# Two-layer graph network on one core: the turn of x by DMA transposes of f16 halves, handed on to the second attention

## The reference

```
def _L0_gnn_ref(src, adj_matrix, ...):
    ...
    x = _ln(src + attn_out, g1, beta1)
    ff = jax.nn.gelu(x @ W1 + b1, approximate=False) @ W2 + b2
    return _ln(x + ff, g2, beta2)

def _L1_gnn_ref(features, adj, Wq, Wk, Wv, Wffn, g1, b1, g2, b2):
    q = heads(features @ Wq)
    k = heads(features @ Wk)
    v = heads(features @ Wv)
    e = jnp.einsum('whqd,whkd->whqk', q, k)
    e = jnp.where(e >= 0, e, ALPHA * e)
    attn = jax.nn.softmax(jnp.where(adj[:, None] > 0, e, NEG), axis=-1)
    h = jnp.einsum('whqk,whkd->whqd', attn, v)
    h = h.transpose(0, 2, 1, 3).reshape(w, n, H * DH)
    out = _layernorm(h, g1, b1)
    out = jnp.concatenate([out, features], axis=-1) @ Wffn.T
    out = _layernorm(out, g2, b2)
    return out + features
```

## Time and profile before

| | us |
|---|---|
| median of 3 runs | 3217.97 |
| lowest, highest | 3217.51, 3224.02 |
| the profiled execution | 3219.48 |
| its span in the trace | 3217.7 |
| stretch of the feed-forward (first load to last store) | 1197 to 1919 |
| stretch of the second attention | 1922 to 3217 |

### The profile page before, as it was taken

How to read it: one execution, slowest core, us unless ns; L and a number is a source line. 1 busy time by engine, 2 the same in 40 slices (tenths; PEclk the granted TensorE clock), 3 DMA queues, 4 the chain that set the end, 5 groups by cost and what they waited for, 6 DMA issues and landing times. The chain is left out here.

```text
span 3217.7 us, 75464 instructions
## 1 busy us (share of the span) xinstructions
PE 3034.0 (94%) x27976; PEld 2081.9 (65%) x28165; DVE 2451.6 (76%) x6789; ACT 1998.5 (62%) x3727; POOL 1679.2 (52%) x1510
## 2 busy tenths in 40 slices
PE   6999999999999949999999977999999999999996
PEld 4666666666666626666666655777777777777774
DVE  5888888888888855565555545888888888888883
ACT  3566656656666535566556644777777777777774
POOL 1555545555555542344344442666666666666665
PEclk8999999999999979999999989999999999999998
DMA  5444444444444421111111113444444444444441
GB/s 156 140 133 136 141 129 147 128 142 134 136 140 134 135 73 37 46 53 49 44 53 53 40 60 121 138 133 146 140 137 142 133 141 142 142 140 133 140 135 45
DMA packets 290744, 365.69 MB, mean 114 GB/s; under 512 B 31680, under 2 KB 199232, under 8 KB 290368
## 3 DMA queue, kind: packets, MB, share of 16 engines
q1 hardware_dynamic: 289216, 359.25, 36.5%
q10 hardware_dynamic: 1152, 1.52, 0.2%
HBM read 242.16 MB, written 118.49 MB: 112 GB/s over the span
## 5 line engine op out<-in xcount | busy, mean ns | idle before, releaser
L2445 DVE TENSOR_TENSOR f_gl<-f_act,f_gh 128x512 f16<-128x512 f32 x256 | 245.3, 959 | 285.2 <-ACT f_act L2367 285.2
L1844 ACT ACTIVATE b_prob<-b_score_t 128x512 f32<-128x512 f32 x512 | 304.2, 594 | 248.5 <-PE b_score_t L2107 248.4
L2034 DVE CUSTOM_DVE_ANT_0 b_junk<-b_score,b_mask 128x256 bf16<-128x256 f32 x1024 | 390.2, 418 | 40.8 <-issue 40.6
L1408 DVE TENSOR_TENSOR a_linked<-a_prob,a_mask 128x1024 f32<-128x1024 f32 x256 | 356.5, 1393 | 2.3 <-ACT a_prob L1205 2.2
L1928 POOL TENSOR_TENSOR b_half_sum<-b_prob 128x512 f32<-128x512 f32 x256 | 335.3, 1310 | 43.6 <-ACT b_prob L1844 43.4
L2362 ACT ACTIVATE f_gh<-f_up,s_f_b 128x512 f16<-128x512 f32 x256 | 175.5, 685 | 280.4 <-PE f_up L2493 280.3
L1205 ACT ACTIVATE a_prob<-a_score_t 128x1024 f32<-128x1024 f32 x256 | 259.3, 1013 | 109.6 <-PE a_score_t L1488 102.7
L1916 POOL TENSOR_TENSOR b_nw_root<-b_nw_var,b_minus_halves 128x2 f32<-128x2 f32 x128 | 112.9, 882 | 407.0 <-DVE b_nw_neg_mean L1975 407.0
L1401 DVE TENSOR_REDUCE a_neg_max<-a_score 128x4 f32<-128x1024 f32 x256 | 307.1, 1199 | 3.9 <-PE a_score L1501 3.8
L1850 ACT ACTIVATE b_score_t<-b_score_t 128x512 f32<-128x512 f32 x512 | 305.8, 597 | 0.3 <-PE b_score_t L2116 0.3
L2491 PE MATMUL f_down<-s_w,f_gh 128*128 128x256 f16 x1024 | 279.1, 273 | 1.0 <-DVE f_gl L2445 1.0
(11 more groups left out here) (235 smaller groups left out, 9205.3 us busy)
## 6 DMA issues: line engine op xcount, KB each, us to landing
a_stack<-qk_scratch SPq DMA_DIRECT2D x384, 128.0 KB, 3.0
b_stack<-qk_scratch SPq DMA_DIRECT2D x384, 128.0 KB, 2.8
qk_scratch<-a_qk SPq DMA_DIRECT2D x64, 512.0 KB, 2.9
qk_scratch<-b_qk SPq DMA_DIRECT2D x64, 512.0 KB, 2.8
a_x_sb<-x_t SPq DMA_DIRECT2D x64, 256.0 KB, 3.2
a_adj_sb<-adj_t SPq DMA_DIRECT2D x64, 256.0 KB, 3.1
a_res<-x_nodes SPq DMA_DIRECT2D x64, 256.0 KB, 3.4
after_attention<-a_z_out SPq DMA_DIRECT2D x64, 256.0 KB, 2.5
```

Source lines behind the costliest of these rows:

```text
L1408: nc.vector.tensor_tensor(linked[:, k], prob[:, k], mask[:, be[1] % 2].unsqueeze(1).to_broadcast([P, 2, NT * N]), ALU.mult).then_inc(link_ ...
L1844: nc.scalar.activation(prob[:, he], score_t[s][:].rearrange("p t n -> p (t n)"), ACT.Exp, scale=ALPHA).then_inc(exp_done, 1)
L2034: last = nc.vector.tensor_tensor_reduce(junk[:, s, it], score[s][:, it], mask[:, i, it], -1.0, 3e38, ALU.add, ALU.min, neg_max[:, i, col:c ...
L2445: nc.vector.tensor_tensor(gl[:, bu[1] % 2, f], act32[:, f % 2], gh[:, bu[1] % 2, f], ALU.subtract).then_inc(low_done, 1)
```

## The change

In the feed-forward, x is no longer turned on PE. ACT makes the high half of the unturned x in SBUF (`xnh`, slot 1) and DVE the low half (`xnl`, slot 1), both laid out as 8 blocks of 128x128. SP turns each with one DMA transpose (128 x 1024, f16, SBUF to SBUF) into `xh` and `xl`. x is loaded one step earlier than before. PE waits at slot 0 for both transposes.

A stage is added to the pipeline (bz, t-4; 36 steps instead of 35). In it ACT and DVE split the result z_out into halves (`znh`, `znl`, slot 2), SP turns them with two more DMA transposes into `zt`, waits for these and stores `zt` in two DMAs to a new HBM tensor, after_layer_0_turned. The f32 result is still stored.

The second attention loads this tensor (256 KB for a batch, both halves) straight into `x_halves` at 4, and has no xT, xh and xl. q waits for the load and for the v of the batch before. The sum of an out row that used a turn bank (`turn[0]`) has a PSUM bank of its own, and one small copy moved on DVE.

```diff
-    AT = {"load": 4, "load_adj": 4, "xT": 8, "xh": 8, "xl": 9, "q": 10, "q_hi": 10, ...
+    AT = {"load": 4, "load_adj": 4, "q": 10, "q_hi": 10, ...
...
-                        if (n := after(back(bx, XS), 4, 1)) is not None:
-                            sp.wait_ge(proj_done, n)
-                        sp.dma_start(x_sb[:, i], rows(x_in, bx)).then_inc(x_loaded[i], 16)
+                        if (n := after(back(bx, XB), 1, 1)) is not None:
+                            sp.wait_ge(out_done, n)
+                        sp.dma_start(x_halves[:, bx[1]].rearrange("p k c n -> p k (c n)"), x_turned[number(bx)]).then_inc(x_loaded[i], 16)
...
-                    if bx := due(t, h, "xT"):
...
-                                pe.wait_ge(xl_ready, count(bp, 1, 1))
+                                pe.wait_ge(x_loaded[bp[1] % XS], uses(bp, XS) * 16)
+                                if (n := after(back(bp, 1), 1, 1)) is not None:
+                                    pe.wait_ge(v_ready, n)
...
@@ feed_forward, SP @@
+                for bl in ((bx, back(t, -1)) if number(t) == 0 else (back(t, -1),)):
+                    if have(bl):
+                        i = bl[1] % 4
+                        if (n := after(back(bl, 4), 1, 1)) is not None:
+                            sp.wait_ge(xb_ready, n)
+                            sp.wait_ge(xnl_ready, n)
+                        sp.dma_start(x_sb[:, i].rearrange("p (g t) n -> p g (t n)", g=G), pair_rows(x_in, bl)).then_inc(x_loaded[i], 16)
                 if have(bx):
-                    i = bx[1] % 4
-                    if (n := after(back(bx, 4), 1, 1)) is not None:
-                        sp.wait_ge(xb_ready, n)
-                    sp.dma_start(x_sb[:, i].rearrange("p (g t) n -> p g (t n)", g=G), pair_rows(x_in, bx)).then_inc(x_loaded[i], 16)
+                    i = bx[1] % 2
+                    if (n := after(back(bx, 2), FC, FC)) is not None:
+                        sp.wait_ge(up_done, n)
+                    sp.wait_ge(xnh_ready, count(bx, 1, 1))
+                    sp.dma_start_transpose(xh[:, i].rearrange("p d n -> p (d n)").rearrange("p (g n) -> p g n", n=P),
+                                           xnh[:, i].rearrange("p d t n -> p (d t n)")).then_inc(x_turned[i], 16)
+                    sp.wait_ge(xnl_ready, count(bx, 1, 1))
+                    sp.dma_start_transpose(xl[:, i].rearrange("p d n -> p (d n)").rearrange("p (g n) -> p g n", n=P),
+                                           xnl[:, i].rearrange("p d t n -> p (d t n)")).then_inc(x_turned[i], 16)
+                if have(bz):
+                    i = bz[1] % 2
+                    if have(back(bz, 2)):
+                        sp.wait_ge(zt_stored[i], uses(back(bz, 2), 2) * 32)
+                    sp.wait_ge(znh_ready, count(bz, 1, 1))
+                    sp.dma_start_transpose(zt[:, i, 0]..., znh[:, i]...).then_inc(z_turned[i], 16)
+                    sp.wait_ge(znl_ready, count(bz, 1, 1))
+                    sp.dma_start_transpose(zt[:, i, 1]..., znl[:, i]...).then_inc(z_turned[i], 16)
...
                     sp.wait_ge(affine, count(bn, 2, 2))
                     sp.dma_start(pair_rows(x_out, bn), ...).then_inc(out_stored[i], 16)
+                if have(bz):
+                    i = bz[1] % 2
+                    sp.wait_ge(z_turned[i], uses(bz, 2) * 32)
+                    for k in range(2):
+                        sp.dma_start(turned_out[...], zt[:, i, k]).then_inc(zt_stored[i], 16)
...
@@ feed_forward, PE @@
-                            pe.wait_ge(xl_ready, count(bu, 1, 1))
+                            pe.wait_ge(x_turned[i], uses(bu, 2) * 32)
...
-                    if f == 4 and have(bx):
...
-                                last = nc.tensor.transpose(turn[d][:, tt * P:(tt + 1) * P], x_sb[:, bx[1] % 4, tt, d * P:(d + 1) * P], ident[:])
```

More of the change, by code:

```diff
@@ L2294, in feed_forward @@
         nw = norm_scratch(ctx, nc, "f_nw", TT)
-        turn = [psum(f"turn{i}", [P, TOK]) for i in range(DC)]
+        row = psum("row", [P, 512])
         up = [psum(f"up{i}", [P, TOK]) for i in range(2)]
@@ L2318, in run @@
         def run(eng, step):
-            for n in range(PAIRS + 3):
+            for n in range(PAIRS + 4):
                 step((n // U, n % U))
@@ L2411, in step @@
                     i = bx[1] % 4
-                    pool.wait_ge(turned, count(bx, 1, 1))
+                    pool.wait_ge(x_loaded[i], uses(bx, 4) * 16)
                     if (n := after(back(bx, 4), TT, TT)) is not None:
@@ L2523, in step @@
                         pe.wait_ge(prep, 3)
[L2524 removed]
                         for d in range(DC):
[L2526 removed]
+                            last = nc.tensor.matmul(row[:, 0:D], shift_wide[:, d], stage[:, HEADS_W, d], start=d == 0, stop=d == DC - 1)
                         last.then_inc(row_made, 1)
[L2528 to L2537 removed]
             run(pe, step)
```

126 lines of the change are left out of this document (64 added, 62 removed).

## The result

| | before | after |
|---|---|---|
| median in the paired runs, us | 3217.74 | 3195.61 |
| lowest of after, highest of after (4 runs) | | 3195.04, 3201.24 |
| ratio, 95% interval | | 0.9931 [0.9914, 0.9949] |
| span of the profiled execution | 3217.7 | 3193.5 |
| first load of the second attention, from the span's start | 1922.00 | 1901.81 |

The account below looks back on a forecast made before the run. PE was taken to bound the feed-forward and its chain the second attention. 3219.5 - 27.8 - 27.3 + 0.8 + 7.4 = 3172.6, forecast as 3171 us, 1.5% faster; likeliest range 3155 to 3195, wider range 3155 to 3400.

Parts of the forecast that it names:

- The feed-forward's turn, 27.8 us: Feed-forward: 8 transposes off PE save 0.87 us in each of 32 steps, 27.8 us; step 21.71 becomes 20.84.
- the new work of ACT and DVE is hidden: Feed-forward: ACT to some 14.4 us, DVE to 14.0 of 20.84 per step, costed at nothing; 10 us if not covered.
- c, the price of a transpose: Feed-forward: SP and queue time per DMA transpose, taken as 2 us; free in the steady state up to 4.2 us.
- rivals 1 and 2: Slow transposes make SP's queue the bound: about 3405 us at 6 us each (0.16), or about 3980 (0.14 with what lies between).
- rival 2: Each 128x128 block costs a transfer of its own, 10.4 us per transpose: about 3980 us; chance 0.14 with what lies between.
- Head +0.8 and tail +7.4: Feed-forward's ends: first up product 0.8 us later for the turned x, and 7.4 us for the added last step.
- The second attention, 27.3 us: Second attention: 4 transposes off PE save 0.44 us in each of 62 batches, 27.3 us.
- Is something late next there?: Second attention: check whether a neighbour holds PE; ACT's relu leaves 1.1 us of slack, so PE may move 0.44 us earlier.
- At the stage's head nothing is won: Second attention's start: no gain, since q is held by the mask work (adj_t, `linked`, the count), not by x.
- number 3: ACT or DVE overrun, c between 4.2 and 4.5, or relu, add and exp hold the second attention: 3195 to 3211; 0.08.
- the second attention's batch at 18.6 us: Sign of being right in the profile after: one batch of the second attention takes 18.6 us, from 19.06.
- the wait for relu (L2107, now L2094): Sign for part of the gain: in the second attention this PE wait grows by what the turn gave.

Follow-up runs that it names:

- x_only: Kernel before with only the feed-forward's x turned by DMA; z neither split nor stored turned, second attention as before: 3193.25 us, ratio 0.9903.
- turns_3x: Changed kernel with each of the four DMA transposes of a feed-forward step issued three times, the extra two into spare buffers: 3224.4 us, single run.
- after_half_late: Changed kernel where POOL's second half_sum of a batch in the second attention also waits for DVE's offset: 3179.65 us, ratio 0.9883.
- ff_all: Changed feed-forward in full, turned z and its stores included, with the second attention of the kernel before: 3200.06 us, ratio 0.9931.
- after_linked6: Changed kernel with DVE's mask operation `linked` due in slot 6 instead of slot 7 of the second attention: 3190.6 us, ratio 0.9895.

## Why the prediction was right or wrong

- **The feed-forward's turn, 27.8 us: right**, step 20.84, PE without waits. So was the claim that the new work of ACT and DVE is hidden, though DVE's was undersized: 418.69 x 20.84 / 550 = 15.9 us a step, where 14.0 were forecast. f_gl went from 959 to 1184 ns in the mean; it has two SBUF inputs, like neg_some, and POOL works beside it. This isn't shown by a run; PE didn't wait for it.
- **c, the price of a transpose: right in kind, 1.25 us of SP instead of 2**, so rivals 1 and 2 fell. With it fell, for this shape, what rival 2 drew from the Trainium skill ("VectorE: DVE Perf Modes", section The three transpose paths): 1309 ns a block, where the traces have 1.25 / 8 = 0.16 us of SP and 0.15 (x_only) to 0.18 us (turns_3x) of the engines.
- **Head +0.8 and tail +7.4: right**, +0.45 from the stage's first load, and 6.9. Up to the second attention's first load the forecast is -27.8 + 0.8 + 7.4 = -19.6, the traces show -20.2.
- **The second attention, 27.3 us: wrong**, and this is the step that failed. "Is something late next there?" was asked of PE's wait for relu alone, with 1.1 us of slack, and for DVE I looked only at its load, which becomes less. But PE waits for DVE at turn_max too, in the slot behind the turn, and the slack there was 0.18 us. It had no row among the waits, since a wait that is only just not there isn't listed. The chain behind it was set by POOL (half_sum) through DVE's neg_some. So 0.17 instead of 0.44 a batch, 17 us less.
- **"At the stage's head nothing is won": wrong in that something was lost**, 4.6 us up to the ninth store. linked, which I took for 1.78 us of work, was a wait for POOL's memset, so adj_t's earlier landing brought nothing. Of the 4.6, 2.7 are the slow batch of the fill, with its longer wait for the load of q and k and the lower clock behind it, and 1.1 the clock at the first k projections, which x_only has too and after_half_late has not: that part isn't shown to come from the change.
- **The rivals**: number 3, "part of the gain: 3195 to 3211", came true in the number, with a mechanism that it named only half (a neighbour in the second attention; it said the relu loop).
- Of the signs to watch for, "the second attention's batch at 18.6 us" failed in the trace, and the sign for it that I had named, the wait for relu (L2107, now L2094), did not grow.

## What to carry to other kernels

When work is taken off the engine that binds, list every wait of that engine in the slot behind it and compute each one's slack from the two timelines, those that the table of waits doesn't show above all: it shows the waits that exist, not those that will come. A small instruction that lasts several times its usual time, and ends with an instruction of another engine, is waiting for it; look at its minimum, median and maximum. Work that is removed may have been covering a chain, and one added wait, in the right place on a third engine, gave back 16 of the 25 us by which the gain had fallen short. And a difference between two traces at the start of a stage isn't yet an effect of the change: a third and a fourth trace showed the same clock, high and low, in both kernels.

## What the runs showed of the hardware

- A DMA transpose of 128x1024 f16 within SBUF holds SP for 1.25 us and takes 1.2 us of all 16 DMA engines (x_only) to 1.46 us (at share 1.00). Their share rises from 0.15 to 0.27 by two of them in 20.84 us, and to 0.47 by four with two stores of 256 KB.
- DVE's neg_some, 128x16 f32 with two SBUF inputs, lasts 0.17 us alone and 0.47 to 0.77 us beside POOL's half_sum, and ends 0.03 us behind that one (median). DVE's linked, 128x512 int32 to f16, lasts 0.43 us without POOL's memset and 3.77 to 3.89 us where it starts 3.3 to 3.4 us behind the memset's start, ending 0.3 us behind it (after, x_only, ff_all, after_linked6, after_half_late).
- After 27 us without work PE's granted clock is 0.50 at the start of the second attention. In after it stays there for 30 us; in after_linked6 and after_half_late, with the same idle time and the same first products, it is at 1.00 from 12 us on. With 24 transposes in that gap the q projections, 6 us into the stage, run at the upper level in all four kernels that have them. A wait of 2.02 us in the fill is followed by a granted clock of 0.57 for 4 us, one of 0.93 us by none lower than 1.00.
